# A chunked delta rule on one core: its small blocks solved by substitution on VectorE, and the gate weights' split moved to the next stage

## What is computed

```
M = tril(-(beta*wk @ wk.T) * L_mask, -1)        # strictly lower, C x C
A = inverse of (I - M)
intra = tril(rk @ wk.T * L_mask, -1)
per chunk: v_new = A @ v_scaled - A @ wk_scaled_decayed @ S
           o = rk_decayed @ S + intra @ v_new
           S = chunk_decay * S + wk_tail.T @ v_new
out = x + o @ W_read.T
```

## Time and profile before

| what | us |
|---|---|
| median of 3 runs | 2561.7 (2559.56 to 2564.49) |
| the profiled execution's own time | 2558.84 |
| its span in the profile | 2557.1 |
| granted TensorE clock, mean | 0.984 |
| busy: PE, DVE, ACT, POOL | 2461.3, 1972.1, 1645.3, 1189.9 |
| PE's load of weights (PEld) | 2060.9 |

### The profile page before, as it was taken

One profiled execution on the slowest core, in us unless ns is written; L12 is line 12 of the kernel. 1 busy time (PEld: TensorE's weight loads), 2 busy tenths in 40 slices (PEclk: granted clock), 3 DMA queues, 4 the chain that ended last, 5 costly groups with the idle time before them and its releaser, 6 DMA issues.

```text
span 2557.1 us, 40983 instructions
## 1 busy us (share of the span) xinstructions
PE 2461.3 (96%) x14724; PEld 2060.9 (81%) x14724; DVE 1972.1 (77%) x3028; ACT 1645.3 (64%) x2578; POOL 1189.9 (47%) x758
## 2 busy tenths in 40 slices
PE   6999999999999999999799999999999999999997
PEld 4999999899999999988576777767777687776876
DVE  6776676555665666577798998989989889898996
ACT  5455554444444444566678778787787777877774
POOL 2224565100000000541576776767767577676774
PEclk9999999999999999999899999999999999999999
DMA  4456554344434434452464655646556456565563
GB/s 158 166 193 176 176 165 141 121 154 146 140 128 155 145 130 156 154 180 84 150 213 154 195 194 183 204 157 196 192 188 202 150 196 206 176 197 159 190 207 113
DMA packets 229609, 427.60 MB, mean 167 GB/s; under 512 B 24897, under 2 KB 112641, under 8 KB 229394
## 3 DMA queue, kind: packets, MB, share of 16 engines
q1 hardware_dynamic: 223250, 407.98, 48.6%
q0 software_dynamic: 6144, 16.79, 1.9%
HBM read 347.58 MB, written 77.10 MB: 166 GB/s over the span
## 4 chain that ended last, share of the span: by engine, by line
PE 69%; DVE 16%; ACT 7%; issue 6%; POOL 1%; DMA 1%; DVEq 0%; POOLq 0%; SPq 0%; ACTq 0%
PE pb L1350 14%; PE pb L1328 14%; PE pb L820 10%; DVE pb L1796 9%; PE pb L2100 4%; PE pb L2105 4%; PE pb L1999 4%; DVE UU L1802 3%; PE pb L812 2%; PE pb L2068 2%; PE pb L2126 2%; PE pb L2024 2%; PE pb L2082 2%; PE pb L2087 1%; PE pb L2015 1%
## 5 line engine op out<-in xcount | busy, mean ns | idle before, releaser
L1728 POOL TENSOR_TENSOR UU<-dx,BB 128x1024 f32<-128x1024 f32 x256 | 608.3, 2391 | 266.1 <-PE pb L1999 266.0
L1927 ACT ACTIVATE pb<-dt,al 128x512 f32<-128x512 f32 x512 | 341.5, 685 | 198.9 <-DVE UU L1802 197.7
L1255 DVE TENSOR_TENSOR HL<-HF,HH 128x512 fp32r<-128x512 f32 x248 | 171.6, 692 | 277.4 <-ACT HH L1170 277.3
L1166 ACT ACTIVATE HF<-pb,BU 128x512 f32<-128x512 f32 x248 | 170.5, 687 | 325.1 <-PE pb L1328 325.0
L1802 DVE TENSOR_TENSOR UU<-pb,CC 128x512 f32<-128x512 f32 x512 | 351.3, 686 | 19.4 <-DMA CC<-bcd 1.4
L1796 DVE TENSOR_TENSOR_SCAN pb<-pb,hs,UU 128x512 f32<-128x512 f32 x256 | 328.4, 1283 | 33.1 <-POOL UU L1728 11.7
L1796 DVE TENSOR_TENSOR_SCAN pb<-pb,UU 128x512 f32<-128x512 f32 x256 | 312.7, 1221 | 42.7 <-ACT pb L1927 28.6
L1129 POOL DMA_INDIRECT ya<-yg,sl x32 | 36.6, 1144 | 605.9 <-DMA yg<-YO 562.4
L1350 PE MATMUL pb<-W2h,HH 128*128 128x256 f32 x992 | 287.1, 289 | 0.0
L1999 PEld LDWEIGHTS pb<-ident,UU 128*128 128x128 f32 x2048 | 236.9, 143 | 59.6 <-issue 43.0
L1350 PE MATMUL pb<-W2l,HH 128*128 128x256 f32 x992 | 280.3, 283 | 0.0
(11 more groups left out here) (301 smaller groups left out, 5141.2 us busy)
## 6 DMA issues: line engine op xcount, KB each, us to landing
WH<-fhd SPq DMA_DIRECT2D x176, 512.0 KB, 3.6
BB<-bcd SPq DMA_DIRECT2D x256, 256.0 KB, 4.8
CC<-bcd SPq DMA_DIRECT2D x256, 256.0 KB, 4.7
raw<-in_w1a SPq DMA_DIRECT2D x23, 1024.0 KB, 5.0
raw<-in_w2a SPq DMA_DIRECT2D x23, 1024.0 KB, 7.7
xg<-zt SPq DMA_DIRECT2D x23, 512.0 KB, 6.0
TM<-xg SPq DMA_DIRECT2D x23, 512.0 KB, 8.7
yg<-YO SPq DMA_DIRECT2D x23, 512.0 KB, 3.1
```

The source lines that it names most:

```text
L1166: e.activation(HF[q % 2][:], wbank("h", q)[:], ACT.Silu, bias=BU[i][:, it:it + 1]).then_inc(s_hf, 1)
L1255: e.tensor_tensor(HH[q % 4][1][:], HF[q % 2][:], HH[q % 4][0][:].bitcast(F32), ALU.subtract).then_inc(s_hl, 1)
L1728: e.tensor_tensor(ubuf(n)[:], dx[p][:], BB[n % 4][:].rearrange("p (a m) -> p a m", a=1).to_broadcast([P, 2, 512]), ALU.mult).then_inc(p_u. ...
L1927: e.activation(abank(n, c)[:], dt[p][:, c, :], ACT.Exp, scale=al1[:, 2 * p + c, s:s + 1]).then_inc(c_a.sem, 1)
```

## The change

It does four things.

- **Blocks of 16 by substitution.** `seed` and levels 1 to 3 go (P1 to P3, D1 to D3, t1 to t4). In their place, M of both heads (now one tile `M2`) has its eight 16 x 16 diagonal blocks stored to DRAM (`md`, 8 transfers) and read back (8 transfers) so that every partition of a block holds the block's 15 rows (`MB`). DVE then solves all 8 matrices in 31 small instructions (`solve`, in two portions, 0 to 11 and 12 to 30) and spreads the result into the block-diagonal `DT` (`inverse`, times a mask). PE turns it once (d4), ACT copies it to `Dm`, and levels 4 to 6 are as before.
- **Order.** The lists of all engines in the loop are rewritten: v, kq, kk, the decays and M of the coming chunks are made one or two chunks ahead; ACT makes the differences (4 activations a tile with a bias) that DVE made; `Ea` is written in place. The last unit's weights (L792, L412) are split after the last chunk instead of inside it.
- **The gate's weights** move to stage b, one block in each of units 1 to 22: ACT rounds at step 2 and sums at step 4, POOL subtracts, SP loads and stores. The flag is made at units 24 and 25.
- **Zero fills**: 16 of 23 go beside the stores of `xrow` in the first norm, two after each; 7 follow the first chunk's blocks.

```diff
-        order = ["kq", "P1", "t1", "D1", "v", "P2", "t2", "D2", "wkT", "P3", "t3", "D3", "wkS", "P4", "t4", "D4",
-                 "P5", "t5", "D5", "P6", "t6", "T6", "vn", "rkT'", "o", "kk'", "S", "MT'"]
+        ahead = ["rkT", "z", "kk", "MT", "v", "kq", "rkT'"]
+        order = ["kk'", "wkT", "d4", "wkS", "P4", "D4", "P5", "t5", "D5", "P6", "t6", "T6", "MT'", "vn", "rkT''", "v'", "o", "S", "kq'"]
...
SP:
             for q in range(8):
                 e.wait_ge(s_ln, 4 * q + 4)
                 e.dma_start(xrow[:, 4 * q:4 * q + 4, :], XS[:, 4 * q:4 * q + 4, :]).then_inc(s_row, 16)
+                zeros(2 * q, 2 * q + 1)
...
+            def blocks(n):
+                for h in range(2):
+                    e.wait_ge(*g_dve[h].at("M", n))
+                for q in range(8):
+                    e.dma_start(md[n, 16 * q:16 * q + 16], M2[16 * q:16 * q + 16, :, :, 16 * q:16 * q + 16]).then_inc(s_md, 16)
+                e.wait_ge(s_md, 128 * (n + 1))
+                if n:
+                    e.wait_ge(*g_x.at(30, n - 1))
+                for q in range(8):
+                    e.dma_start(MB[16 * q:16 * q + 16].rearrange("p r g c -> p (r g c)"),
+                                md[n, 16 * q + 1:16 * q + 16].rearrange("(o r) h b c -> o (r h b c)", o=1).to_broadcast([16, 1920])).then_inc(s_mb, 16)
...
+            sums(1); blocks(0); zeros(*range(16, NU))
             for n in range(NSEQ):
+                if n + 1 < NSEQ: blocks(n + 1)
+                if n: residuals(n - 1)
+                if n + 2 < NSEQ: sums(n + 2)
+                if 4 <= n < 7: reload(4 * n - 12, 4 * n - 11, 4 * n - 10)
...
+                if 3 <= n < 7: reload(4 * n - 9)
POOL:
+            lower(0); upper(0); decayed(0); lower(1)
             for n in range(NSEQ):
+                upper(n + 1); scatter(chunk_pairs(n, 0)); scatter(chunk_pairs(n, 1))
+                lower(n + 2); decayed(n + 1); scatter(chunk_pairs(n, 2))
DVE:
+            def solve(n, steps):
+                for k in steps:
+                    r = (k - 1) // 2
+                    if k == 0:
+                        e.wait_ge(s_mb, 128 * (n + 1))
+                        e.tensor_copy(X16[:], eye[:]...)
+                    elif k % 2:
+                        e.tensor_tensor(Y16[:, :, r:15], MB[:, r:15, :, r].rearrange("p r g -> p g r"),
+                                        X16[:, :, r:r + 1].to_broadcast([P, 8, 15 - r]), ALU.mult)
+                    else:
+                        e.tensor_tensor(X16[:, :, r + 1:16], X16[:, :, r + 1:16], Y16[:, :, r:15], ALU.add)
...
             for n in range(NSEQ):
+                residual_a(n - 1); mix(n + 1, h); (R: the 8 of L646)
+                for l in (4, 5, 6): level(l, n)
+                norms(n + 2); (vnt); values(n + 1, h); solve(n + 1, range(12))
+                (S: the 8 of L665); inner(n + 1, h); solve(n + 1, range(12, 31)); inverse(n + 1, h)
ACT:
             for n in range(NSEQ):
+                wk; d4; upper(n + 1); decays; carried(n + 1); t5; t6; MT(n + 1); vn
+                turned_rows(n + 2); lower(n + 2); o; squares and roots(n + 3)
+            for l in range(2):
+                e.wait_ge(s_w0, 32)
+                e.activation(WB[0][2 * l][:], fview[l], ACT.Copy).then_inc(s_w0h, 1)
Stage b, ACT:
+                if u in weights and it == 2:
+                    e.wait_ge(s_craw, 16 * (c + 1))
+                    e.activation(chi_b[:], craw_b[:], ACT.Copy).then_inc(s_chi, 1)
+                if u in weights and it == 4:
+                    e.wait_ge(s_clo, c + 1)
+                    e.activation(craw_b[:], clo_b[:].bitcast(F32), ACT.Abs, accum_out=cnt[:, c:c + 1]).then_inc(s_cnt, 1)
```

More of the change, by code:

```diff
@@ new lines, in sums_of, with await_sums, lower @@
+            def sums_of(n, h):
+                return ZR[h] if n else gbank("z", 0, h)[:].rearrange("p (b m) -> p b m", b=4)
+            def await_sums(n, h):
+                if n:
+                    e.wait_ge(s_zr, 16 + 32 * n)
+                else:
+                    e.wait_ge(*g_pe[h].at("z", 0))
+            def lower(n):
+                for h in range(2):
+                    W, z_ = TB[h], sums_of(n, h)
+                    await_sums(n, h)
+                    if n:
+                        e.wait_ge(*g_dve[h].at("M", n - 1))
+                    for b in range(4):
+                        t = e.activation(W["E"][:, b, :], z_[:, b, :], ACT.Relu, bias=sm["ncum"][:, n + 8 * b, h:h + 1])
+                    t.then_inc(g_act[h].sem, 1)
@@ L755, in copy @@
                     e.activation(TB[h][to][:], four(gbank(bank, n, h)), ACT.Copy).then_inc(g_act[h].sem, 1)
[L757 to L765 removed]
+            turned_rows(0)
+            e.wait_ge(*a_dve.at("ncum"))
+            lower(0)
@@ new lines, in roots @@
+            def roots(n):
+                e.wait_ge(s_sq, 8 * n + 8)
+                e.activation(rn[:, n:NT:8, :], rn[:, n:NT:8, :], ACT.Sqrt).then_inc(s_rnq, 1)
+            for b in range(4):
+                squares((1 + 8 * b,))
+            roots(1)
+            copy("MT", 0, "MT", "MT")
+            carried(0)
+            for b in range(4):
+                squares((2 + 8 * b,))
+            roots(2)
+            turned_rows(1)
+            lower(1)
+            for n in range(NSEQ):
+                more = n + 1 < NSEQ
+                copy("wk", n, "wkT", "wk")
+                copy("d4", n, "d4", "Dm")
+                if more:
+                    upper(n + 1)
+                    decays(n + 1, "ET")
+                    decays(n + 1, "ez")
+                    carried(n + 1)
+                if n == 1:
+                    e.wait_ge(*r_dve.at("pd"))
+                    e.activation(p2[:], p2[:], ACT.Exp, scale=0.5).then_inc(r_act.sem, 1)
+                copy("t5", n, "t5", "DT")
+                copy("t6", n, "t6", "DT")
+                if more:
+                    copy("MT", n + 1, "MT", "MT")
@@ L948, in pe_a @@
                     product("vn", n, h, W["DT"], W["vsc"])
[L949 to L950 removed]
+                if n + 2 < NSEQ:
+                    rkT(n + 2)
+                if more:
+                    values(n + 1)
                 for h in range(2):
@@ L1016, in program @@
         LB = NU + NB - 1
+        weights = {u + 1: u for u in range(NCH)}
+        UF = NCH + 2
         front_pe = {**{(LB - 4 + c, 3): [("in", 0, c)] for c in range(4)}, (LB, 5): [("xp", 0, 0)], (LB, 6): [("dt", 0, 0), ("dt", 0, 1)]}
```

545 lines of the change are left out of this document (312 added, 233 removed).

## The result

The kernel after takes 2522.29 us (median, 2520.66 to 2524.27), the one before 2561.89 in the same runs: ratio 0.9848 (95% interval 0.9836 to 0.986), **39.6 us less** where 76 were forecast. The profiled execution has a span of 2522.5 us against 2557.1. The page, as the earlier trace rows: engine, busy time, share; granted clock; chain of waits.

A forecast was written before the change was run, and what follows sets the result against it. PE was taken to bound the kernel, busy 96% of the span. Start 93 + 2, loop 7 x 39.6, scatter 8 and end 35.3 put the first unit product at 415.5 against 489.7, giving 2486 us, range 2458 to 2532.

The forecast's parts named there:

- PE's work in a chunk, 36.7: Delta-rule loop: six product pairs and three turn pairs go, leaving PE 36.7 us a chunk, 14.0 less.
- the low end plus 0.8 us a chunk: VectorE's substitution in the loop: element part 8.0 to 10, spreads 1.8 to 3; low end taken, plus 0.8 for POOL contention.
- The round trip, 20 us, hidden: M2 to DRAM and back as MB: 20 us, hidden within 22.6 us between M(n+1) and the substitution.
- Rivals 1 and 2: Round trip does not fit, 25 to 30 us: 2509 to 2533, chance 0.21; slower, 38 us: 2605, chance 0.05.
- rival 4: Better: round trip 14 us or less and no hold by the scatter: 2465, chance 0.13.
- Scatter, 8 us: Chunks 4 to 6: POOL waits for reloaded rows ahead of lower(n + 2), so M(n + 2) is late; 8 us together (0 to 20).
- The start: P4 of chunk 0 moves from 84.5 to 93 as nothing covers the round trip: 8.5 us, plus 2 for lower clock.
- rival 5: Zero fills run late, at half the rate, moving all of chunk 0 by 15 to 25 us: 2505, chance 0.05.
- The end, 35.3: From P4 of chunk 7 to the first unit product: 35.3 us, including 11.0 for unit 0's weights split after OT.
- Stages b and c, 0: Later stages keep their length; the gate's weight split fits into idle ACT, POOL and DMA time in stage b: cost 0.
- rival 3: Stage b does not hide the split: second product delayed 1.2 us in 22 units, 26 us: 2512, chance 0.06.
- the period: Loop length per chunk: PE's 36.7 plus waits and contention gives 39.6 us instead of 53.5, longer in chunks 4 to 6.

The follow-up runs named there:

- e4_light: Kernel after, with POOL's passes over E cut to 8 elements from chunk 2 on (M is another matrix): 2554.6 us, 0.9826 of the kernel before.
- e11_eact: e10_w0 with OT ahead of E on ScalarE, E's mask dropped and its nbeta scale moved from POOL to ScalarE: 2541.3 us, 0.9779 of the kernel before.
- e1_act: Kernel after, with ScalarE copying OT(n) ahead of E(n + 2): 2564.6 us, 0.9853 of the kernel before; unchanged control 0.9856.
- e2_pool: Kernel after, with POOL's masks of E(n + 2) and rkdT(n + 1) ahead of the scatter's first two parts: 2582.1 us, 0.9935 of the kernel before.
- e13_fills: Kernel after, with the zero fills moved back into the loop, behind ZR's pair in chunks 0 to 2: 2561.7 us, 0.9834 of the kernel before.
- e10_w0: Kernel after, with unit 0's weights loaded before chunk 6's residual stores and split inside chunk 7, ScalarE's copies behind d4: 2553.5 us, 0.981 of the kernel before.
- e7_nosplit: Kernel before, without the split of the gate's weights in stage a, its stores writing zeros: 2608.9 us, 1.003 of the kernel before.

## Why the prediction was right or wrong

- **PE's work in a chunk, 36.7.** The count was right (no instruction too many), the time was not: 39.2 busy. The low clock was counted once, 2 us at the start; it came back in every chunk, behind PE's new waits, and cost 17.3 us over seven. This is the largest single term that was mis-sized. That the waits bring the low clock is read from the order of events; no run varied it by itself.
- **VectorE and POOL.** The sum of VectorE's work was right, 34.0 against 33. The substitution alone takes 8.6 with the copy, forecast 8.0. What was wrong is "the low end plus 0.8 us a chunk, because POOL is idle during the second portion": POOL meets the first portion, whose instructions are the longest, and takes 3.5 to 4.2 us (e4_light and e11_eact: 1.9 without E's passes). With it, d4 waited 18.0 us for DT over the loop, where 1 to 1.5 a chunk were counted, 7 to 10.5.
- **A wait that no step named.** ScalarE's order puts E(n + 2), and so the landing of ZR, ahead of OT(n): 10.4 us of PE. I had listed what SP and POOL queue behind a wait, and not what ScalarE does. e1_act shows d4 waiting for DT where y no longer waits.
- **The round trip, 20 us, hidden.** (The sum of the start has 22 for it, without a reason.) It took 16.0: the second M ends at 59.7 and the copy of `eye` begins at 75.8; the stores and the wait took 6.4 (forecast 6.9), the reads 9.5 (forecast 13.1). From chunk 1 on, VectorE never waits for MB. The price taken from BB's row was too high. Rivals 1 and 2 are out, and rival 4's 14 us were not reached. The estimate by the Trainium skill (SBUF — State Buffer, "Door 1: The DMA port swizzle"), 9 us for the read and 18 in all, is the nearer one, and still too slow: less 1.8 to land, the 0.98 MB took 7.7 us with their issues, 128 GB/s (an estimate from these rows), more than a quarter of 435.

```profile
59.05 0.69 DVE L533 TENSOR_TENSOR M<-pb,E 128x512 f32<-128x512 f32 x1 [1.00 <-POOL E L401]
66.26 3.58 SPq L310 DMA_DIRECT2D MB<-md  x8
75.76 0.23 DVE L542 COPY X<-eye 128x128 f32<-128x128 f32 x1 [6.52 <-DMA MB<-md]
```

- **Scatter, 8 us.** M's waits are 9.8: right in place and size. Its obvious cure is not one on the chips tried (e2_pool).
- **The start.** P4 of chunk 0 at 91.5, forecast 93 (90 to 97) and 2 for the clock: right by terms that cancel. The round trip took 16.0 for the 22 of that sum. The substitution took 10.3 for 8.0, as POOL's passes over E(1) lie beside it, and from its end to P4 it took 5.4 us for 2.3: wkS stands there, 3.1 us, and the sum left it out. No cost of the fills can be told (e13_fills), and rival 5 is out.
- **The end, 35.3.** 40.1. The weights' part was right to 0.1 us (10.9); POOL's drain behind it was missing, 5.3 us, though the trace of before has it, and e10_w0 shows the whole place to be worth about 12.
- **Stages b and c, 0.** 1.0 and 1.2 us: right, rival 3 is out. The split's removal from stage a was worth nothing in the kernel before (e7_nosplit), and the sum gave it nothing.

The direction and the mechanism held: PE lost the work of three levels, the round trip was hidden, and the split cost nothing in stage b. The sum was 37 us short, 36 of them in the loop's length, so about half of the forecast gain came. The 2522.3 us lie outside the forecast's own range (2474 to 2500). They lie inside the wide one (2458 to 2532) only because rivals 1, 3 and 5 stretched it, and none of the three happened: that is luck. Two of the things that were to show the forecast right did not: the period (45.9 for 39.6) and the small instructions (up to 1.16 us for 0.2 to 0.3).

## What to carry to other kernels

When a bounding engine loses a quarter of its work, forecast its new waits first: the longer ones were also followed by the low clock, and both terms together were as large as half the forecast gain. Chains of small VectorE instructions on two SBUF tiles take the length of whatever POOL runs beside them, so put POOL's passes next to VectorE's PSUM work, and cut those that nothing reads. And when an order is rewritten, list for each engine, ScalarE too, what stands behind an operand that comes by DMA.

## What was not expected of the hardware

- POOL's drain at the end of the stage ends 5.3 us behind POOL's last pass in every trace, the two kernels' and the variants'. Its whole length, 12.53 to 12.61 us in the kernel after and its variants and 9.87 in the kernel before, includes what is left of the passes. The drains of ScalarE and VectorE take 0.2 to 0.8 us when nothing is left before them.
- On three chips the same kernels take 1.5% longer, and PE waits 17.4 us for "issue" in the loop, nearly all while POOL issues indirect transfers; on the first chip the kernel after has no such wait, and the kernel before has 10.8 us outside the scatter's runs. What holds PE's signals back was not found.
- An instruction on 8 elements of two SBUF tiles takes 0.17 us, on 120 elements 0.28 to 0.36.
- ZR's pair lands 12 to 16 us after its issue when MB's eight transfers are ahead of it, and 10.0 before the change.
